# One and two 512-column products of constants ahead of every group's sums in the two gathers of a graph, expert and LSTM kernel

## What is computed

```python
h_all = jnp.einsum('nd,rdo->rno', xn, W_r)                    # first graph layer, 16 relations
msg = h_all[edge_type, src] / deg[edge_type, dst][:, None]
x = x + segment_sum(msg, dst) + xn @ W0_w.T + W0_b
...
h = xn @ W                                                    # second graph layer, with self loops
out = segment_sum(dinv[src] * dinv[dst] * h[src], dst) + b
x = x + leaky_relu(out)
```

## Time and profile before

| | first gather | second gather | whole |
|---|---|---|---|
| stretch of the profile, us | 800 to 2022 | 2539 to 3715 | 0 to 4460.6 |
| PE busy, us | 967.7 | 746.3 | 3620.2 |
| DVE busy, us | 499.2 | 396.2 | 1892.6 |
| POOL busy, us | 756.1 | 770.6 | 1689.3 |
| granted TensorE clock, share of 2.4 GHz | 0.73 | 0.79 | 0.856 |
| share of the DMA engines | 0.41 | 0.41 | |

### The profile page before, as it was taken

How to read it: one execution, slowest core, us unless ns; L and a number is a source line. 1 busy time by engine, 2 the same in 40 slices (tenths; PEclk the granted TensorE clock), 3 DMA queues, 4 the chain that set the end, 5 groups by cost and what they waited for, 6 DMA issues and landing times. The chain is left out here.

```text
span 4460.6 us, 61216 instructions
## 1 busy us (share of the span) xinstructions
PE 3620.2 (81%) x19537; PEld 2807.0 (63%) x19537; DVE 1892.6 (42%) x5872; ACT 913.0 (20%) x2407; POOL 1689.3 (38%) x1769
## 2 busy tenths in 40 slices
PE   7999999577888877877999644566766778999996
PEld 3444444576777767765666444454555557999996
DVE  4555300233344444553555421223344445444687
ACT  2333333000000111112333200000000002444554
POOL 1000000566666666652222366766666660000000
PEclk9999999667767777788999866777788899999998
DMA  4333444333344444443333323334344544433333
GB/s 148 150 152 152 158 169 162 105 94 101 111 116 124 131 127 132 144 131 120 114 115 114 105 84 92 112 113 123 123 139 143 157 153 146 154 126 119 109 109 112
DMA packets 240339, 567.38 MB, mean 127 GB/s; under 512 B 44899, under 2 KB 130428, under 8 KB 226191
## 3 DMA queue, kind: packets, MB, share of 16 engines
q1 hardware_dynamic: 150912, 319.30, 20.7%
q0 software_dynamic: 85344, 238.92, 18.0%
q10 hardware_dynamic: 3760, 5.24, 0.3%
HBM read 371.44 MB, written 191.42 MB: 126 GB/s over the span
## 5 line engine op out<-in xcount | busy, mean ns | idle before, releaser
L918 POOL DMA_INDIRECT a_msg<-scratch_hrel,k_rel_row x782 | 758.1, 969 | 432.8 <-issue 213.3
L1642 POOL DMA_INDIRECT b_msg<-scratch_gx,k_src_row x782 | 770.6, 985 | 388.6 <-issue 228.1
L992 PE MATMUL a_ps<-a_hit,a_msg 128*128 128x128 f32 x3128 | 580.2, 352 | 151.3 <-issue 103.0
L704 PE MATMUL r_psm<-k_w,r_xnT 128*128 128x512 f32 x1568 | 693.2, 597 | 4.9 <-ACT r_hst L668 4.0
L1693 PE MATMUL b_ps<-b_hit,b_msg 128*128 128x128 f32 x3128 | 482.7, 315 | 214.0 <-issue 112.5
L992 PEld LDWEIGHTS a_ps<-a_hit,a_msg 128*128 128x128 f32 x3128 | 520.5, 255 | 202.1 <-issue 137.7
L1693 PEld LDWEIGHTS b_ps<-b_hit,b_msg 128*128 128x128 f32 x3128 | 460.3, 228 | 267.3 <-issue 154.0
L2096 PE MATMUL l_psg<-k_hall,k_whhT 128*128 128x125 f32 x4640 | 550.5, 277 | 5.2 <-DVE k_hall L2222 5.2
L2096 PEld LDWEIGHTS l_psg<-k_hall,k_whhT 128*128 128x128 f32 x4640 | 538.1, 193 | 5.7 <-DVE k_hall L2222 5.7
L704 PEld LDWEIGHTS r_psm<-k_w,r_xnT 128*128 128x128 f32 x1568 | 293.0, 191 | 348.6 <-issue 340.6
L1797 DVE TENSOR_TENSOR k_accT<-k_accT,b_ps 128x256 f32 x196 | 82.5, 421 | 636.6 <-DMA a_typ<-scratch_typ 445.3
(11 more groups left out here) (276 smaller groups left out, 3692.8 us busy)
## 6 DMA issues: line engine op xcount, KB each, us to landing
scratch_hrel<-r_hst SPq DMA_DIRECT2D x98, 1024.0 KB
l_xr<-scratch_xrow SPq DMA_DIRECT2D x146, 512.0 KB, 3.4
scratch_xrow<-n_xs SPq DMA_DIRECT2D x50, 512.0 KB
a_msg<-scratch_hrel,k_rel_row POOLq DMA_INDIRECT x782
b_msg<-scratch_gx,k_src_row POOLq DMA_INDIRECT x782
n_xb<-scratch_gx SPq DMA_DIRECT2D x48, 256.0 KB
scratch_xtab<-g_xn SPq DMA_DIRECT2D x49, 132.0 KB
scratch_x<-n_xo SPq DMA_DIRECT2D x50, 128.0 KB
```

Source lines behind the costliest of these rows:

```text
L704: mm = pe.matmul(psm[:, c % 4], xnT[:, u, kk], k.w[:, kk, c * 512:(c + 1) * 512], start=(kk == 0), stop=(kk == 1))
L918: pool.indirect_dma_start(msg[:, q, j], None, table, bass.IndirectOffsetOnAxis(ap=rows_of[:, g, j:j + 1].bitcast(U32), axis=0)).then_inc(s ...
L992: mm = pe.matmul(ps[:, u, kk, 0:WIN], msg[:, g % SL, j, kk * P:(kk + 1) * P], hit[:, u, j], start=(j == 0), stop=(j == pieces(g)[-1]))
L1642: pool.indirect_dma_start(msg[:, q, j], None, rows_of, bass.IndirectOffsetOnAxis(ap=k.src_row[:, g, j:j + 1].bitcast(U32), axis=0)).then_i ...
```

## The change

In both gathers PE makes products of constants between the wait for the bank and the wait for the messages: one of 512 columns in the first gather, two in the second. They write the bank that the group's sums then start anew, so their values are used by nobody. Operands are the identity and weights that lie in SBUF anyway. Nothing else is changed; the branch for scattered edges (`scan`) stays as it was.

```diff
@@ stage_first
+                    def busy(u):
+                        for _ in range(1):
+                            pe.matmul(ps[:, u].rearrange("p k c -> p (k c)"), k.ident[:],
+                                      k.w0[:].rearrange("p k d -> p (k d)"), start=True, stop=True)
+
                     def sums(g):
                         u = g % 2
                         pe.wait_ge(s_p, g + 1)
                         if g >= 2:
                             pe.wait_ge(s_add, g - 1)
+                        busy(u)
                         for j in pieces(g):
                             pe.wait_ge(s_m[g % SL][j], 16 * (g // SL + 1))
                         for kk in range(2):
@@ stage_second
+                    def busy(u):
+                        for _ in range(2):
+                            pe.matmul(ps[:, u].rearrange("p k c -> p (k c)"), k.ident[:],
+                                      wT[:, 0, 0:4].rearrange("p g d -> p (g d)"), start=True, stop=True)
+
                     def sums(g):
                         u = g % 2
                         pe.wait_ge(s_p, g + 1)
                         if g >= 2:
                             pe.wait_ge(s_add, g - 1)
+                        busy(u)
                         for j in pieces(g):
                             pe.wait_ge(s_m[g % SL][j], 16 * (g // SL + 1))
                         for kk in range(2):
```

## The result

Slower by little: 4533.0 us (median of 5 runs, 4527.0 to 4546.1) against 4502.7 us of before beside it (4493.0 to 4506.4). The ratio is 1.0074, with a 95% interval of 1.0058 to 1.0090: +30.3 us, outside the 0.2% that would count as no change. The forecast of 4542 us and its own range (4506 to 4620) hold it.

What follows compares the result with a forecast made beforehand. The prediction took POOL's waits for late news of finished sums in the two gathers as the bound. First gather +10 and second +35 us on 4497 gave 4542 us, range 4470 to 4620, the likeliest case's own 4506 to 4620.

Steps and rivals of the forecast that it cites:

- What bounds before: Both gathers: POOL pauses 198 and 154 us on late news of sums; products, behind the bank wait, delay sums.
- Shorter stretches: Both gathers: products delay sums, so POOL makes fewer calls between pauses, mostly 8 or 12; 4506 to 4620 us, chance 0.60.
- The 6.5 us: Both gathers: sums completed within about 6.5 us of POOL's resumption are seen at once, later ones mostly when POOL stops.
- First gather +10: First gather: stretches of three groups become two, +23 us, against a gain by the clock; +10 us taken.
- Second gather +35: Second gather: five-group stretches shorten to three or four, 6.06 against 5.88 us per group over 195.5 groups, +35 us.
- The 6.06 us per group: Second gather: price per group with products, taken between those of three-group and two-group stretches, against 5.88 us now.
- All other stages only begin later: Outside the two gathers: the other stages were said to start later only, with no time added to the sum.
- The clock pays: Rival, first gather: runs at nearly full clock (above about 0.9), gaining up to 53 us; 4444 to 4488 us, chance 0.20.
- Hidden: Rival, gathers: most completions wait for POOL's stop anyway, so the delay costs nothing; 4488 to 4506 us, chance 0.12.
- PE as the bound: Rival, gathers: clock stays low and PE sets the pace; +280 us, 4777 us, or a third, 4680 us; chance 0.08.
- Products: Sign, both gathers: the added products take 0.44 to 0.89 us per record and nothing waits for messages.

Runs made afterwards that it cites:

- again: The changed kernel run once more with no edit, against the kernel before the change: 4503.4 against 4472.5 us, ratio 1.0074.
- g1_only: The change's product kept only in the first gather, none in the second, against the kernel before the change: 4476.8 against 4467.3 us, ratio 1.0019.
- g2_only: The change's two products kept only in the second gather, none in the first, against the kernel before the change: 4495.5 against 4467.3 us, ratio 1.0063.
- slow288: Kernel before the change, no products, plus a 288-column memset behind every POOL call in both gathers: 4459.0 against 4472.5 us, ratio 0.9972.
- slow288_products: The changed kernel plus a 288-column memset behind every POOL call in both gathers, against the kernel before the change: 4459.6 against 4472.5 us, ratio 0.9975.
- double: Twice the change's products, two in the first gather's groups and four in the second's, against the kernel before the change: 4626.5 us, ratio 1.0346.
- mixed: Kernel before the change, no products, plus memsets behind POOL's calls, 264 columns in the first gather, 240 in the second: 4402.1 against 4465.0 us, ratio 0.9855.

## Why the prediction was right, and where not

- *What bounds before.* Confirmed: POOL's pauses end on late news, 0.8 us after a late update of `s_mm`. PE's products are not hidden, because nothing is left to wait for ahead of the sums; but where the trace names PE's last wait in the second gather it is the one for `hit`, not the bank wait of the prediction. Both stand ahead of the products, so the argument holds. The prediction could not say why news is late. The runs show what it hangs on: POOL's distance between calls (second gather: late updates 115 of 177 at 1.26 us, 114 of 169 at 1.29, 0 of 162 at 1.48).
- *Shorter stretches.* Confirmed: 81 to 91 and 97, 50 to 61 and 63 stretches; mostly 8 and 12 calls in the first gather (42 and 27 of the 91 stretches of again) and 12 in the second (29 of 61). POOL's pauses exceed 198 and 154 us as forecast, with 230 and 175 in the first profile; in again they are 214 and 157, so in the second gather the sign is weak.
- *The 6.5 us.* This step failed as put: "at least one prompt completion of each five-group stretch is lost". In the second gather's stretches of at least 8 calls, 0.96 adds per stretch were prompt in before, 1.09 in again and 0.89 in the first profile of the change. The first add after a resumption came 5.5 us behind it and now 5.9 (medians), not 6 to 8. What the runs show instead is that a stretch holds 782 / 4 / 61 = 3.2 groups instead of 3.9 at the same count of prompt adds, while PE's groups follow each other in 3.5 us instead of 1.8. That the shorter stretches come from groups that PE finishes too late in one is my reading; no run varies it alone.
- *The terms.* First gather +10: again's profile shows 15.2 - 2.1 = 13. Second gather +35: 11.1 within the calls and 9.5 behind the last, 21. The 6.06 us per group behind the +35 measured 1161.4 / 195.5 = 5.94 in again and 6.02 in the first profile. "All other stages only begin later" left the second part out. The sum, 45 predicted, is 32.7 in that profile and 30 to 31 in the medians. That it came so near has luck in it: the price within the second gather was put at three times what again shows, which made up for the end that was left out, and the +10 was a choice between +23 and a gain by the clock. That g1_only has 9.5 and g2_only 28.2 in the medians fits the order of the two terms; their profiles do not show it.
- *The clock pays*: its condition was not met, the first gather's clock was 0.86 and not 0.9. Both gathers had a higher clock and were longer, as the forecast said. Where POOL is spaced out the products raise the mean clock of the execution from 0.861 (slow288) to 0.937 (slow288_products), and the time is the same. The rule of the Trainium skill (TensorE: Matmul & The Clock Gate, "What's actually happening"), that activity releases the throttle, agrees with the rise from 0.73 to 0.86; it does not follow that time is gained, since PE's speed was not the bound.
- *Hidden* was wrong for this kernel. With POOL spaced out by 288 columns the products cost 0.6 us, but by another way than this rival's: they fit into PE's wait for messages.
- *PE as the bound* needs four products in the second gather (double).
- *Products* at 0.44 to 0.89 us per record: by busy time, as the 0.44 was worked out, 259.6 / 392 = 0.66 and 411.0 / 784 = 0.52 (the records overlap, so their mean lengths are 0.75 and 0.65). Nothing waited for messages: right.

## What to carry to other kernels

Work put "between two waits" costs nothing only if the second wait is the one that ends last; look in the trace who waits for the messages before calling the time idle. A higher granted clock is no gain where the engine is not the bound. And where an engine stalls on news that is late, look at what the issuing engine does at that time: here spacing POOL's gathers from 1.26 to some 1.45 us per call made the kernel 1.45% faster (mixed).

## What was not expected of the hardware

- The updates of PE's `s_mm` come late while POOL issues indirect gathers 1.26 us apart (up to 27.4 us behind the products' end in before), and 0.01 us behind it in the median at 1.48 us. DVE's updates of `s_add` are on time in both cases. The messages do not fall behind either: their last packet ends 2.4 us (first gather) and 2.7 us (second) after the call's start for the first call of a stretch of before and 2.4 us for the twentieth (medians by place in the stretch 2.3 to 2.8 us). The delay lies between the products' end and the update; which part of the chip holds the update back no run here shows, nor why the first gather's edge lies higher (late updates 134 of 187 at 1.44 us in the median, 51 of 175 with 264 columns, 1 of 159 at 1.48) than the second's.
- A memset of 64 columns on POOL behind each gather (0.17 us) lengthens the distance by only 0.03 us; one of 288 columns (0.37 and 0.35 us) by 0.22.
